# Cross-attention block on one core: x transposed in 64-row halves among the probabilities, and steps 0 to 2 written in another order

## What is computed

```python
h = _layernorm(x, gamma, beta)
Q = (h @ Wq).reshape(B, NQ, N_HEADS, HEAD_DIM)
K = (context @ Wk).reshape(B, NC, N_HEADS, HEAD_DIM)
V = (context @ Wv).reshape(B, NC, N_HEADS, HEAD_DIM)
attn = jnp.einsum('bihd,bjhd->bhij', Q, K)
attn = jax.nn.softmax(attn, axis=-1) * scale
vals = jnp.einsum('bhij,bjhd->bihd', attn, V).reshape(B, NQ, INNER)
out = vals @ Wo + bo
return x + out
```

## Time and profile before

| | |
|---|---|
| median of 3 runs | 331.27 us (331.06 to 331.31) |
| the profiled execution's own time | 331.32 us |
| its span (first to last instruction of the trace) | 329.3 us |
| PE busy | 319.2 us, 97% of the span |
| DVE busy | 253.8 us, 77% |
| ACT busy | 253.2 us, 77% |
| POOL busy | 155.5 us, 47% |

### The profile page before, as it was taken

How to read it: one execution, slowest core, us unless ns; L and a number is a source line. 1 busy time by engine, 2 the same in 40 slices (tenths; PEclk the granted TensorE clock), 3 DMA queues, 4 the chain that set the end, 5 groups by cost and what they waited for, 6 DMA issues and landing times.

```text
span 329.3 us, 9691 instructions
## 1 busy us (share of the span) xinstructions
PE 319.2 (97%) x3773; PEld 281.7 (86%) x3773; DVE 253.8 (77%) x587; ACT 253.2 (77%) x798; POOL 155.5 (47%) x289
## 2 busy tenths in 40 slices
PE   5998999999999999999999999999999999999985
PEld 5877888998888899888899888889888889988874
DVE  4888877877878777786887778787787877668784
ACT  4898988787778777788778877777878877777862
POOL 4675677534663166342554336632465415333330
PEclk9999999999999999999999999999999999999999
DMA  6980000020000300020000200003000000000000
GB/s 178 262 255 3 0 2 3 2 91 0 2 3 2 90 1 2 2 76 15 3 3 1 90 2 2 2 1 91 2 2 2 20 15 2 2 2 33 2 3 32
DMA packets 10860, 10.70 MB, mean 33 GB/s; under 512 B 960, under 2 KB 10304, under 8 KB 10816
## 3 DMA queue, kind: packets, MB, share of 16 engines
q1 hardware_dynamic: 10336, 9.77, 9.9%
q10 hardware_dynamic: 416, 0.33, 0.3%
q0 software_dynamic: 64, 0.00, 0.1%
HBM read 8.00 MB, written 2.10 MB: 31 GB/s over the span
## 4 chain that ended last, share of the span: by engine, by line
PE 88%; ACT 5%; DVE 3%; POOL 2%; issue 1%; DVEq 0%; POOLq 0%; ACTq 0%
PE mix_ps L870 16%; PE ring_ps L841 13%; PE o_ps L978 12%; PE ring_ps L936 12%; PE ring_ps L894 10%; PE ring_ps L1015 9%; PE ring_ps L1052 8%; PE ring_ps L1059 3%; ACT prob L461 3%; PE ring_ps L914 1%; PE o_ps L802 1%; PE mix_ps L815 1%; PE mix_ps L807 1%; DVE prob_t L783 1%; DVE qk_lo L686 1%
## 5 line engine op out<-in xcount | busy, mean ns | idle before, releaser
L370 POOL TENSOR_SCALAR prob<-prob,inv 128x256 f32<-128x256 f32 x192 | 89.0, 480 | 106.1 <-DVE inv L668 105.9
L461 ACT ACTIVATE prob<-ring_ps,neg_max 128x256 f32<-128x256 f32 x256 | 118.1, 474 | 21.4 <-DVE neg_max L661 21.4
L661 DVE TENSOR_REDUCE neg_max<-ring_ps 128x2 f32<-128x512 f32 x128 | 81.3, 678 | 0.6 <-PE ring_ps L841 0.6
L870 PE MATMUL mix_ps<-prob_t,v_sb 128*64 128x256 f32 x504 | 61.5, 386 | 0.5 <-DVE prob_t L783 0.5
L686 DVE TENSOR_TENSOR qk_lo<-ring_ps,qk_hi 128x512 fp32r<-128x512 f32 x64 | 44.2, 691 | 17.7 <-ACT qk_hi L471 17.6
L783 DVE COPY prob_t<-ring_ps 128x512 f32<-128x512 f32 x64 | 41.2, 686 | 21.0 <-PE ring_ps L1015 21.0
L461 ACT ACTIVATION_READ_ACCUMULATOR prob<-ring_ps,neg_max 128x1 f32 x256 | 52.8, 206 | 0.0
L471 ACT ACTIVATE qk_hi<-ring_ps 128x512 fp32r<-128x512 f32 x64 | 38.7, 604 | 14.1 <-PE ring_ps L936 14.1
L870 PEld LDWEIGHTS mix_ps<-prob_t,v_sb 128*64 128x64 f32 x504 | 33.5, 137 | 18.3 <-issue 0.6
L841 PE MATMUL ring_ps<-qk_hi 64*128 64x256 f32 x256 | 39.5, 301 | 0.4 <-DVE qk_lo L686 0.3
L1015 PE MATMUL ring_ps<-ident,prob 64*128 64x64 f32 x1024 | 37.5, 223 | 1.0 <-DVE prob L676 1.0
(11 more groups left out here) (129 smaller groups left out, 687.2 us busy)
## 6 DMA issues: line engine op xcount, KB each, us to landing
x_in<-in_x_dram SPq DMA_DIRECT2D x8, 256.0 KB, 3.1
out_dram<-y_sb SPq DMA_DIRECT2D x7, 256.0 KB, 2.2
c_in<-in_ctx_dram SPq DMA_DIRECT2D x7, 192.0 KB, 3.0
w_raw<-in_L_xattn_Wq_dram SPq DMA_DIRECT2D x8, 128.0 KB, 3.3
w_raw<-in_L_xattn_Wo_dram SPq DMA_DIRECT2D x4, 256.0 KB, 4.8
w_raw<-in_L_xattn_Wk_dram SPq DMA_DIRECT2D x4, 128.0 KB, 3.6
w_raw<-in_L_xattn_Wk_dram SPq DMA_DIRECT2D x8, 64.0 KB, 3.4
w_raw<-in_L_xattn_Wv_dram SPq DMA_DIRECT2D x2, 256.0 KB, 4.9
```

The costliest lines, as they stand in the source:

```text
L370: last = nc.gpsimd.tensor_scalar(prob[:, e, r, :], prob[:, e, r, :], inv[:, e, r:r + 1], SCALE, ALU.mult, ALU.mult)
L461: last = nc.scalar.activation(prob[:, e, r, :], score_bank(u, e)[:, r * ROWS:(r + 1) * ROWS], ACT.Exp, bias=neg_max[:, e, r:r + 1], accum_ ...
L661: nc.vector.tensor_reduce(neg_max[:, e, :], score_bank(u, e)[:, :].rearrange("p (r j) -> p r j", r=RT), AX, ALU.max, negate=True).then_inc ...
L870: last = nc.tensor.matmul(ps[h * HALF:(h + 1) * HALF, first:first + ROWS], v_sb[:, w // RT % 2, j, p * P + h * HALF:p * P + (h + 1) * HALF ...
```

## The change

Seven edits, in the order of the program:

1. Start-up: 2 + 8 idle transposes instead of 6 + 6. x 0 is turned by row tiles, each after its own half of the normalization (`x_norm_first`). On DVE the wide part of `context_lo(0)` goes ahead of `norm(0)`. ACT makes `h_hi` of tile 0 straight from PSUM, ahead of `h_full`.
2. Step 0, PE: the low key products of pairs 2 and 3 stand between the two halves of `scores(0)`. `values(0)` and `values(1)` run high parts first, then low parts.
3. Step 1, DVE: `weight_lo(13)` moves behind the first two `maximum`, `context_lo(1)` behind the last two, and the second half of `norm(1)` behind `last_head`.
4. Step 1, ACT: `context_hi(1)` moves behind `probabilities(1)`, `weight_hi(15)` to the end of the step's heads.
5. Step 1, POOL: it waits for the scaling of head 3 on DVE before `weight_lo(15)` and the next ones.
6. Step 2: piece 19 is split on DVE (ahead of `mix_lo`) instead of POOL.
7. Steps 5, 9, ..., 25: x is not turned by four transposes of 128 rows ahead of `values`, but by eight of 64 rows inside the first half of `turn(u)`. ACT's `hidden` moves with it, from ahead of the value copy to between the two copies of turned heads.

The diff, without the declarations and the parts that only rename:

```diff
-    LO_VECTOR = (0, 4, 5, 9, 13, 20, 21)
-    LO_POOL = (1, 2, 3, 6, 7, 8, 10, 11, 12, 14, 15, 16, 17, 18, 19, 22, 23)
+    LO_VECTOR = (0, 4, 5, 9, 13, 19, 20, 21)
+    LO_POOL = (1, 2, 3, 6, 7, 8, 10, 11, 12, 14, 15, 16, 17, 18, 22, 23)
...
+        def x_inside(u):
+            return of_seq(u, TURN_X, 2)
+        def x_is_turned(engine, b):
+            engine.wait_ge(x_turned, min(b, 1) + 1)
+            if b >= 2:
+                engine.wait_ge(x_turned_half, 2 * (b - 1))
...
@@ POOL, step(u)
-                        if e == 1 and u == 2:
-                            weight_lo(19)
+                if u == 1:
+                    pool.wait_ge(scaled_vector, u + 1)
                 for n in {0: (10, 11, 12), 1: (15, 16, 17, 18)}.get(u, ()):
                     weight_lo(n)
@@ ACT, ahead of the steps
+            nc.scalar.activation(h_hi[:, 0, 0, :], x_banks[0][:, 0:ROWS], ACT.Identity,
+                                 bias=beta_c[:, 0:1], scale=gamma_c[:, 0:1])\
+                .then_inc(h_hi_first, 1)
             nc.scalar.activation(h_full[:, 0, :], x_banks[0][:, 0:ROWS], ACT.Identity,
...
-            act.wait_ge(h_full_ready, 1)
-            nc.scalar.activation(h_hi[:, 0, 0, :], h_full[:, 0, :], ACT.Copy)\
-                .then_inc(h_hi_first, 1)
@@ ACT, step(u)
                 if u == 1:
                     weight_hi(14)
-                    act.wait_ge(c_turned, 2)
-                    context_hi(1, context_bank(1))
...
                 probabilities(0)
                 probabilities(1)
-                if u in (1, 2):
-                    weight_hi({1: 15, 2: 19}[u])
+                if u == 1:
+                    act.wait_ge(c_turned, 2)
+                    context_hi(1, context_bank(1))
+                if u == 2:
+                    weight_hi(19)
...
                 if u == 1:
+                    weight_hi(15)
                     weight_hi(16)
...
                     for e in range(0, HEADS, 2):
-                        act.wait_ge(turned, HEADS * u + e + 1)
+                        act.wait_ge(turned, HEADS * u + e + 1 + (e == 0 and x_inside(u) is not None))
                         nc.scalar.activation(turned_half(e), score_bank(u, e)[:, :]
...
+                        if e == 0 and x_inside(u) is not None:
+                            turned_x_out(x_inside(u))
@@ DVE, ahead of the steps
             statistics(0)
             weight_lo(0)
+            dve.wait_ge(c_hi_ready, 1)
+            context_lo_wide(0, context_bank(0))
             norm(0)
-            context_lo(0, context_bank(0))
+            context_lo_narrow(0, context_bank(0))
@@ DVE, step(u)
                 maximum(0)
                 maximum(1)
                 if u == 1:
-                    context_lo(1, context_bank(1))
+                    weight_lo(13)
                 maximum(2)
                 inverse(0)
                 maximum(3)
                 inverse(1)
+                if u == 1:
+                    context_lo(1, context_bank(1))
...
+                if u == 2:
+                    weight_lo(19)
...
                 keys_lo(0)
-                if u == 1:
-                    norm(1, (1,))
...
                 if u < 2:
                     last_head()
+                if u == 1:
+                    norm(1, (1,))
                 keys_lo(1)
...
                     if u == 0:
                         deviation_base(1)
-                        weight_lo(13)
@@ PE, scores(u), between a = 0 and a = 1
+                    if u == 0 and a == 1:
+                        for k in range(BATCH):
+                            keys(BATCH + k, k, parts=(1,))
@@ PE, turn(u)
+                def of_x(k, half):
+                    d, r = divmod(k, RT)
+                    own = slice(half * HALF, (half + 1) * HALF)
+                    first = d * ROWS + r * P + half * HALF
+                    last = nc.tensor.transpose(mix_ps[:, first:first + HALF],
+                                               x_norm[own, r, d * P:(d + 1) * P], ident[own, own])
+                    if k == DT * RT - 1:
+                        last.then_inc(x_turned_half, 1)
...
+                    if a == 0 and b is not None:
+                        pe.wait_ge(x_norm_ready, b + 1)
+                        for k in range(per_bank + of_x_bank):
+                            if k < of_x_bank:
+                                of_x(k, 0)
+                            else:
+                                of_prob(a, k - of_x_bank, 0)
+                            if k < per_bank:
+                                of_prob(a, k, 1)
+                            else:
+                                if k == per_bank:
+                                    pe.wait_ge(x_turned_half, 2 * (b - 2) + 1)
+                                of_x(k - per_bank, 1)
+                        continue
@@ PE, start-up
-            keep_warm(WARM)
+            keep_warm(WARM // 3)
             pe.wait_ge(c_loaded[0], 16)
             turn_c(0, context_bank(0))
-            keep_warm(WARM)
-            pe.wait_ge(x_norm_ready, 1)
-            turn_x(x_banks, 0)
+            keep_warm(WARM + WARM // 3)
+            for r, norm_done in enumerate((x_norm_first, x_norm_ready)):
+                pe.wait_ge(norm_done, 1)
+                for d in range(DT):
+                    last = nc.tensor.transpose(x_banks[d][:, r * P:(r + 1) * P],
+                                               x_norm[:, r, d * P:(d + 1) * P], ident[:, :])
+            last.then_inc(x_turned, 1)
```

More of the change, by code:

```diff
@@ L512, in step, with turned_x_out @@
                 if u == 1:
+                    weight_hi(15)
                     weight_hi(16)
+                def turned_x_out(b):
+                    act.wait_ge(h_lo_ready, DT * b)
+                    x_is_turned(act, b)
+                    hidden(b, mix_ps)
                 def prepared():
@@ L519, in prepared @@
                         context_hi(b, context_bank(b))
-                    b = of_seq(u, TURN_X, 1)
-                    if b is not None:
-                        act.wait_ge(h_lo_ready, DT * b)
-                        act.wait_ge(x_turned, b + 1)
-                        hidden(b, mix_ps)
+                    if u == 1:
+                        turned_x_out(1)
                     if u == 2:
@@ L1006, in turn, with of_prob @@
             def turn(u):
+                def of_prob(a, k, half):
+                    h, j, r = k // (RT * RT), k // RT % RT, k % RT
+                    own = slice(half * HALF, (half + 1) * HALF)
+                    last = nc.tensor.transpose(
+                        score_bank(u, 2 * a + half)[:, k * HALF:(k + 1) * HALF],
+                        prob[own, 2 * a + h, r, j * P:(j + 1) * P], ident[own, own])
+                    if k == 2 * RT * RT - 1:
+                        last.then_inc(turned, 1)
+                def of_x(k, half):
+                    d, r = divmod(k, RT)
+                    own = slice(half * HALF, (half + 1) * HALF)
+                    first = d * ROWS + r * P + half * HALF
[3 more added lines that the diff above has]
+                        last.then_inc(x_turned_half, 1)
+                b = x_inside(u)
                 for a in range(BATCH):
@@ L1011, in turn, with values @@
                         pe.wait_ge(scaled_vector, u + 1)
-                    for k, (h, j, r) in enumerate(itertools.product(range(2), range(RT), range(RT))):
-                        for half in range(2):
-                            own = slice(half * HALF, (half + 1) * HALF)
-                            last = nc.tensor.transpose(
-                                score_bank(u, 2 * a + half)[:, k * HALF:(k + 1) * HALF],
-                                prob[own, 2 * a + h, r, j * P:(j + 1) * P], ident[own, own])
-                            if k == 2 * RT * RT - 1:
-                                last.then_inc(turned, 1)
-            def values(n):
+                    per_bank, of_x_bank = 2 * RT * RT, DT * RT
+                    if a == 0 and b is not None:
[12 more added lines that the diff above has]
+                        continue
+                    for k in range(per_bank):
+                        for half in range(2):
+                            of_prob(a, k, half)
+            def values(n, part=None):
                 g, j = divmod(n, RT)
@@ L1027, in values @@
                 rows = slice(j * P, (j + 1) * P)
-                if j == 0 and g in FOR_V:
+                if j == 0 and g in FOR_V and part != 1:
                     high_ready(pe, FOR_V[g])
@@ L1037, in values @@
                     for m, (w, i, k) in enumerate(passes):
+                        if part is not None and part != (w is wv_lo):
+                            continue
                         if m == CT and j == 0:
@@ L1043, in values @@
                                                 skip_group_check=True)
-                    last.then_inc(v_made, 1)
+                    if part != 0:
+                        last.then_inc(v_made, 1)
```

(8 more changed lines are left out.)

26 lines of the change are left out of this document (17 added, 9 removed).

## The result

| | before | after |
|---|---|---|
| median (lowest to highest) | 331.31 us (331.06 to 331.33) | 332.94 us (332.25 to 333.25) |
| executions | 5 | 5 |
| span of the profiled execution | 329.3 us | 331.0 us |

The changed kernel is slower: ratio 1.0049, interval [1.0037, 1.0061], so 0.5% or 1.6 us. The forecast was 328.5 us.

A forecast was written before the change was run, and what follows sets the result against it. PE, busy 97% of the span, was taken as the bound. Gains of 1.2 (narrow x), 1.45 (steps 1 and 2) and 0.1 us (start-up) sum to 2.75 us, from 331.32 to 328.57, given as 328.5 us; range 327.4 to 329.9.

The forecast's parts named there:

- ACT's part of the move: Steps that turn x: `hidden` between the two copies of turned heads delays nothing PE needs; cost nothing.
- the cover: ACT's 0.87 us of idle behind the copies, until the next `maximum`, was to absorb the second copy's microsecond of delay.
- Rival D: `hidden` between the copies makes the next `maximum`, exp and scaling late for `turn`: 1 us a sequence, 334.5 us; 3%.
- Narrow x: Steps 5 to 25, six times: 64-row x transposes gain 0.23 us less 0.03 for a wait; 1.2 us, bounds 0 to 1.4.
- Rival B: Steps that turn x: the x halves do not pair or stall, so their gain vanishes; 329.7 us; 11%.
- Steps 1 and 2: Earlier, shorter scaling of head 3 and no wait for weight piece 19: 1.45 us gained, bounds 0.7 and 1.7.
- rival A: Steps 1 and 2: moved waits return, the norm meeting POOL's piece 15 or `wv_lo` becoming the wait; 329.3 us; 16%.
- The reason for the short scaling: Step 1: POOL now waits until head 3's scaling is done, so its two instructions take 0.70 us instead of 1.40.
- Start-up: Fewer idle transposes, a later norm and a shorter cast sum to 0.1 us gained, -0.4 to +0.4.
- Both collisions that were named: Start-up: POOL's pieces may now meet DVE's norm; the cast of 0.76 us, probably long because of POOL, likely gets shorter.
- rival C: Start-up: PE's clock rises later, first keys and queries run at half rate; about 1.2 us lost, 329.7 us; 8%.

The follow-up runs named there:

- run 5: The kernel before with only ACT's `hidden` moved between the two copies of turned heads, x turned as before: 333.9 us, ratio 1.0085.
- run 4: The kernel before with only x turned in 64-row halves among the probabilities, `hidden` moving with it: 334.91 us, ratio 1.0108.
- run 7: The kernel of run 3 with eight small writes put at the start of DVE's program: 329.31 us, ratio 0.9944.
- run 9: The kernel of run 6 with PE waiting for the second `maximum` instead of the first: 337.22 us, ratio 1.0181.
- run 12: The changed kernel once more, unchanged, one profiled execution: 331.44 us.
- run 2: The changed kernel with ACT's `hidden` behind both copies of turned heads instead of between them: 331.3 us, ratio 1.0001.
- run 8: The kernel of run 2 with the first `keys` of the step behind x ahead of `mix`: 331.1 us, ratio 0.9994.
- run 1: The changed kernel with `keys_rest` behind `mix` instead of ahead of it in the step behind x: 330.09 us, ratio 0.9965.
- run 6: The kernel before with PE waiting for the first `maximum` ahead of `keys_rest` in the six steps behind x: 333.73 us, ratio 1.0076.
- run 3: The changed kernel with its start-up and reordered steps 0 to 2 kept, but x turned as before: 329.76 us, ratio 0.9958.
- run 10: The kernel of run 7 without POOL's wait for the scaling of head 3 in step 1: 329.35 us, ratio 0.9944.
- run 11: The kernel of run 7 with the start-up as in the kernel before: 329.51 us, ratio 0.9945.

## Why the prediction was wrong

**The step that failed** is the one on ACT's part of the move: "ACT's part of the move is costed at nothing. [...] PE needs the second copy only in the second half of `mix`, after the scores (1.47 us) and the first half of `mix`." `keys_rest` was forgotten. It stands right behind the scores, writes into the bank that the second copy reads, and waits by name for `prob_t_ready` of both halves. So the second copy is due 1.50 us after the first score (62.36 - 60.86), and it ends 1.79 us after it (71.91 + 0.49 - 70.61). To that come 0.05 us until `keys_rest` starts (72.45) and 0.1 until `mix` does (0.31 instead of 0.21 us behind it). Measured from the first score to `mix`: 0.44 us for each of six sequences, with the narrow x and with the wide one (run 5), 2.6 us against a cost of nothing. For the reader that the prediction had in mind, the second half of `mix`, the copy would have been in time: that is due some 1.71 + 1.88 / 2 = 2.65 us after the first score. The 0.87 us of idle on ACT that was called the cover was real, but it lies behind the copies; what waited was work that needs the copy itself done, and idle time behind a late result hides nothing.

Rival D had the instruction right, `hidden` between the copies, and the place and price wrong: no late `maximum` or scaling at `turn`, but `keys_rest`, at 0.44 us and not 1. By its own bound (2.75 / 6 = 0.46 us a sequence) a price of 0.44 alone would have left about no change. It was given 3%, which was far too little for a mechanism whose reader had not been looked up.

**The second part, 1.8 us, is in no term of the sum**: the slow stretches. Where they come from stays open. What the traces show:
- Within a stretch, the 128-row matmuls of keys, queries, output and values follow each other at 0.1175 instead of 0.1133 us, the scores and `mix` at their usual pace.
- From step 3 on, each one starts between the values of one step and the keys of the next, where the 64-row matmuls of `turn`, `scores` and `keys_rest` stand. It ends there too, in the same or in a later step, unless `turn_c` comes first: in all eight cases in which a slow stretch reached the four 128-row transposes of `turn_c`, the values behind them were at the usual pace again (the changed kernel and run 4 in steps 8, 12 and 20, run 7 in step 4, run 9 in step 8). The stretches behind x in the changed kernel end there:

```profile
96.61 1.42 PE o_ps L1015 x12
...
98.46 0.92 PE ring_ps L1124 x8
```

- It comes in one execution and not in the next of the same program (run 12).
- Of the six steps behind x, with the narrow x, three are slow in the changed kernel, none in run 12, five in run 2, four in run 4, all six in run 8 (where PE waits in none) and none in run 1 (no wait either). With the wide x and a bare wait (runs 5, 6, 9) none of 18 is.
- With the wide x it stands elsewhere: in the output product of step 2 in the kernel before, in step 3 in run 3, in steps 3 and 4 in run 7, and in steps 29 and 30 behind the wait in step 29 (run 3; of the five traces with the narrow x that have this wait, all but run 1).

So a wait of PE is neither needed (run 8) nor enough (runs 5, 6, 9). That the narrow x favours the slow pace is argued from these counts, not shown, and by runs 1 and 12 it isn't enough either.

**The third, 0.3 us,** is the wait for DVE in step 29; steps 29 and 30 at the slower pace, 0.3 us of the 1.8, come with it. Runs 3 and 7 show that it depends on the length of DVE's program ahead of it. The prediction could not have had it from a trace of before.

**What held.**
- Narrow x: forecast 0.20 us for a step (0.23 at best), measured 0.21 to 0.22, so the halves pair and the wait on the own result is covered. Rival B is refuted. But no order tried here keeps this gain: in runs 1 and 8, where the second copy or `mix_ps` is no longer waited for, the next step takes as much longer, by what the moved products cost in their new place (run 1) and with the slower pace on top (run 8). The gain per step was read rightly and its worth was not: 1.2 us forecast, about nothing (330.09 in run 1 against 329.76 in run 3).
- Steps 1 and 2: forecast -1.45, measured -1.81 at the output product of step 2, with the start-up in it (forecast 1.55). The scaling starts at 28.31 and takes 0.61 us (forecast 28.5 and 0.70; it took 1.40):

```profile
28.31 0.61 DVE L707 TENSOR_SCALAR prob<-prob,inv 128x256 f32<-128x256 f32 x2
28.84 0.41 DVE L629 TENSOR_SCALAR x_norm<-x_in,mean_var,rstd 128x256 f32<-128x256 f32 x1
...
29.02 1.51 POOL L320 TENSOR_TENSOR w_lo<-w_raw,w_hi 128x256 fp32r<-128x256 f32 x2 [1.01 <-DVE prob L707]
```

  The second half of `norm(1)` is first and takes 0.41 us, its length alone, though POOL's piece starts 0.18 us behind it, and PE waits neither for it nor for `wv_lo`: rival A is refuted, too. The reason for the short scaling was half wrong: POOL does stay away from it, but without its wait as well (run 10).
- Start-up: forecast 0.1 us, nothing that run 11 can tell. Both collisions that were named are there, one each way:

```profile
6.77 1.14 DVE L629 TENSOR_SCALAR x_norm<-x_in,mean_var,rstd 128x256 f32<-128x256 f32 x2
...
9.35 0.29 DVE L663 CAST h_hi<-h_full 128x256 fp32r<-128x256 f32 x1
```

  The norm now meets POOL's pieces (1.14 us, before 0.73) and the cast no longer does (0.29 us, before 0.76). The Trainium skill (SBUF — State Buffer, "Who interferes with whom") has VectorE and GpSimd share a port pair that one of them holds for a whole instruction; these two pairs of durations, with the scaling's 0.61 against 1.40, agree. The first query starts at 9.83 us instead of 9.90, the keys ahead of it are 0.116 to 0.120 us apart from the second on (in the kernel before the first five are 0.21 us apart and more), and the first scores start at 12.41 instead of 12.52: rival C is refuted.

The version to keep is the reordering alone with the eight writes (run 7, 329.31 us, 0.6% faster than before); run 10 says that its edit 5, and run 11 that its edit 1, may be left out.

## What to carry to other kernels

When an instruction of a helper engine is put between two results, look up every instruction that waits for the later result, by its semaphore and not by its name: here a writer of the bank from which that result was copied, in a function that has nothing to do with probabilities, was due a microsecond before the one that came to mind. Idle time behind a late result is no cover for it. And a gain of 0.2 us in one step of the bound engine is only worth something if the step behind it, measured from start to start, is not longer by as much: the two steps together are what to predict.

## What the runs showed of the hardware

- PE's fp32r matmuls of 128 rows and 128 weight columns (keys, queries, output, values, but not `mix`) have a second, 4% slower pace (0.1175 against 0.1133 us apart), which comes and goes by execution (run 12 against the first profile of the same kernel) and costs 0.16 us a step. The granted clock reads 1.00 at both, but it reads 1.00 in the start-up of the kernel before as well, where the x transposes start 0.213 us apart instead of 0.110 in step 1, so this reading alone doesn't tell a pace. The four 128-row transposes of `turn_c` ended a slow stretch in eight cases of eight.
- An engine can pause 0.43 us between its semaphore instruction and the next one at a place that depends on the length of its program: DVE's idle of 1.18 us in step 29 of run 3 went back to 0.81 when eight writes were put ahead of everything (run 7).
- Transposes of 64 rows in pairs take 0.030 us each, also with x among them: 40 of them take 1.21 us, from 69.40 to the first score at 70.61 (forecast 1.24).
- Two 64-row products between 128-row ones cost 0.31 us from start to start (`keys_rest` in run 1), and 0.12 us where other 64-row products stand ahead of them.
